# Own values by transposes, ranks by one maximum, a moved one-hot and a share of the own scaling on VectorE, in the last stage of a graph network kernel

## What is computed

```
h = relu(layernorm(x))
q = (h @ Wq + bq).reshape(n, DH, H) * DH ** -0.5      # H = 8 heads, DH = 32
k, v = the same with Wk, bk and Wv, bv
s = einsum('edh,edh->eh', q[row], k[col])
e = exp(s - segment_max(s, row)[row])
a = e / segment_sum(e, row)[row]
x = x + segment_sum(a[:, None, :] * v[col], row).reshape(n, -1) @ Wo + bo
```

## Time and profile before

| | |
|---|---|
| time, median of 3 runs | 3628.44 us (3624.29 to 3637.78) |
| span of the profiled execution | 3555.4 us |
| PE busy | 3183.0 us, 90% |
| DVE busy | 2914.9 us, 82% |
| ACT busy | 2651.2 us, 75% |
| POOL busy | 1969.9 us, 55% |
| mean granted clock of PE | 0.958 |

### The profile page before, as it was taken

The page is one execution under the profiler, slowest core; times in us unless marked ns, Lnnn a source line. Parts: engine busy times, 40 slices in busy tenths (PEclk is TensorE's granted clock), DMA queues, the critical chain, the costliest instruction groups (busy, mean ns, idle before and its releaser), DMA issues. The chain is left out here.

```text
span 3555.4 us, 83958 instructions
## 1 busy us (share of the span) xinstructions
PE 3183.0 (90%) x21026; PEld 2603.3 (73%) x21026; DVE 2914.9 (82%) x8060; ACT 2651.2 (75%) x7851; POOL 1969.9 (55%) x1669
## 2 busy tenths in 40 slices
PE   1699999699998289999999999947999999999998
PEld 0355554477776278888888888836999999999998
DVE  8788887588875378888888888847999999999996
ACT  0688888599997467777777777726888888888886
POOL 0344444155554387777777777725555555555552
PEclk6799999899999689999999999978999999999999
DMA  1455555488886478888888888737666666666663
GB/s 33 145 203 203 201 201 193 175 306 308 307 306 253 166 265 309 310 309 309 308 308 309 308 309 308 290 125 237 236 232 232 232 237 234 233 232 234 233 237 110
DMA packets 335632, 861.24 MB, mean 242 GB/s; under 512 B 98483, under 2 KB 152922, under 8 KB 323018
## 3 DMA queue, kind: packets, MB, share of 16 engines
q1 hardware_dynamic: 241082, 678.75, 53.4%
q0 software_dynamic: 66256, 78.94, 7.5%
q10 hardware_dynamic: 28224, 102.77, 7.1%
HBM read 521.95 MB, written 416.52 MB: 264 GB/s over the span
## 5 line engine op out<-in xcount | busy, mean ns | idle before, releaser
L2191 ACT ACTIVATE e_mine<-e_mine,e_attention 128x32 f32<-128x32 f32 x3136 | 684.8, 308 | 57.8 <-DVE e_attention L2329 57.5
L1715 PE MATMUL c_qkv_ps<-w_qkv_lo,c_ht_hi 128*128 128x256 f16 x2352 | 642.0, 273 | 0.0
L1715 PE MATMUL c_qkv_ps<-w_qkv_hi,c_ht_hi 128*128 128x256 f16 x2352 | 642.0, 273 | 0.0
L1715 PE MATMUL c_qkv_ps<-w_qkv_hi,c_ht_lo 128*128 128x256 f16 x2352 | 641.9, 273 | 0.0
L2146 POOL DMA_INDIRECT e_kv<-kv_table,e_near x392 | 420.9, 1074 | 127.9 <-issue 100.8
L1607 POOL DMA_INDIRECT c_got<-y_table,c_near x392 | 395.0, 1008 | 110.0 <-issue 95.1
L2138 POOL TENSOR_TENSOR e_kv<-e_kv,e_part_of 128x1024 f32<-128x1024 f32 x98 | 188.2, 1921 | 411.2 <-DVE e_part_of L2352 411.2
L2206 PE MATMUL e_out_ps<-w_out,e_mean_t 128*128 128x256 f32 x1568 | 392.8, 380 | 0.0
L776 POOL DMA_INDIRECT dst_slots<-dst_word,dst_goal x240 | 236.6, 986 | 267.5 <-ACT a_hn L812 189.9
L846 PE MATMUL a_h_ps<-a_ht,w_t 128*128 128x512 f32 x784 | 360.8, 603 | 25.1 <-ACT h L794 21.5
L1109 PE MATMUL mix_ps<-w_mix,hb 128*128 128x256 f32 x1568 | 358.1, 382 | 21.2 <-ACT hb L1078 21.2
(11 more groups left out here) (425 smaller groups left out, 8143.7 us busy)
## 6 DMA issues: line engine op xcount, KB each, us to landing
kv_table<-c_kv SPq DMA_DIRECT2D x98, 1024.0 KB, 6.7
h_table<-h ACTq DMA_DIRECT2D x98, 512.0 KB, 2.6
h<-h_table SPq DMA_DIRECT2D x98, 512.0 KB, 4.2
y_table<-y_out ACTq DMA_DIRECT2D x98, 512.0 KB
agg_table<-agg_out SPq DMA_DIRECT2D x98, 512.0 KB
c_agg<-agg_table SPq DMA_DIRECT2D x98, 512.0 KB, 4.3
x_table<-c_x SPq DMA_DIRECT2D x98, 512.0 KB, 2.7
q_table<-c_q SPq DMA_DIRECT2D x98, 512.0 KB, 4.2
```

Of the source, the lines that this page charges most:

```text
L1715: last = nc.tensor.matmul(qkv_ps[n][:, j * D:(j + 1) * D], h[u][:, kc, j * P:(j + 1) * P], wt[:, kc, n * D:(n + 1) * D], start=m == 0, sto ...
L2191: last = nc.scalar.activation(of_head, of_head, ACT.Copy, scale=attention[u][:, j, h, 0:1])
```

## The change

Four things, all in the last stage but for a constant. (1) In each half of the mean the own values are written first, by matmuls with `is_transpose` against the identity, of which the first opens the accumulation; the gathered values are added behind them. The wait for the gathered values stands between the two loops. (2) The prefixes are made with a new constant `raised_h`: `before_h` with 256 on the diagonal. So a slot's own column holds 256 plus its rank and is the row's maximum, and one `reduce_max` over the four rows takes the place of four products with a sum; `layer` compares with 256 to 263. (3) VectorE's order is new: the one-hot is made a step ahead, behind the ranks; sums of scores and spreading come directly behind the attention, then ranks, the one-hot, and the parts. (4) Of the own scaling the fourth row moves from ScalarE (8 activations) to VectorE (one product of 256 elements behind the attention, with its own semaphore). The lower bound of the total (L2323) is gone. The wait for the seen matmul is now a plain `wait_ge`, that for the state a `hold`.

```diff
+RAISE = 256
...
+                    pool.memset(raised_h[:, :], 1.0).then_inc(raising, 1)
+                    pool.wait_ge(raising, 1)
+                    pool.affine_select(out=raised_h[:, :], in_=raised_h[:, :], compare_op=ALU.is_ge, fill=0.0, base=-1,
+                                       pattern=[[1, P]], channel_multiplier=-1).then_inc(raising, 1)
+                    pool.wait_ge(raising, 2)
+                    pool.affine_select(out=raised_h[:, :], in_=raised_h[:, :], compare_op=ALU.not_equal, fill=float(RAISE), base=0,
+                                       pattern=[[-1, P]], channel_multiplier=1).then_inc(const_ready, 1)
...
-                    dve.wait_ge(const_ready, 19)
+                    dve.wait_ge(const_ready, 20)
...
-                            for j in range(kc * 2, kc * 2 + 2):
+                            for j in range(kc * 2, min(kc * 2 + 2, ROWS - 1)):
...
-                    pe.wait_ge(shared, t + 1)
                     pe.wait_ge(own_shared, t * 2 + 2)
+                    pe.wait_ge(own_last, t + 1)
                     wait_past(pe, mean_t_ready, t * 2 + (kc - 1))
                     for j in range(ROWS):
-                        nc.tensor.matmul(mean_ps[kc][:, j * P:(j + 1) * P], kv[w][:, j, D + kc * P:D + (kc + 1) * P], hot[w][:, j, :],
-                                         start=True, stop=False)
-                        last = nc.tensor.matmul(mean_ps[kc][:, j * P:(j + 1) * P], mine[w][:, j, kc * P:(kc + 1) * P],
-                                                ident[:, :], start=False, stop=True)
+                        nc.tensor.matmul(mean_ps[kc][:, j * P:(j + 1) * P], mine[w][:, j, kc * P:(kc + 1) * P], ident[:, :],
+                                         start=j == 0, stop=False, is_transpose=True, skip_group_check=True)
+                    pe.wait_ge(shared, t + 1)
+                    for j in range(ROWS):
+                        last = nc.tensor.matmul(mean_ps[kc][:, j * P:(j + 1) * P], kv[w][:, j, D + kc * P:D + (kc + 1) * P], hot[w][:, j, :],
+                                                start=False, stop=True, skip_group_check=True)
                     last.then_inc(mean_ready, 1)
...
-                            last = nc.tensor.matmul(prefix_ps[:, j, :], before_h[:, :], hot_h[s][:, j, :], start=True, stop=True)
+                            last = nc.tensor.matmul(prefix_ps[:, j, :], raised_h[:, :], hot_h[s][:, j, :], start=True, stop=True)
...
+                def peaks(at):
+                    t, u = ring_tile(at), at[1] % 2
+                    dve.wait_ge(seen_ready, t + 1)
...
+                def normalise(at):
+                    t, (w, n), u = ring_tile(at), in_ring(at, RING), at[1] % 2
+                    dve.wait_ge(weight_ready, t + 1)
+                    hold(dve, state_loaded[w], n * 16 + 16)
+                    v.tensor_tensor(weight[u][:, :, :, 0], weight[u][:, :, :, 0], state[w][:, :, WEIGHTS:STATE], ALU.mult).then_inc(totalling, 1)
+                    dve.wait_ge(totalling, t * 2 + 1)
+                    v.reduce_sum(total[u][:, :, :], weight[u][:, :, :, :], axis=AX.X).then_inc(totalling, 1)
+                    dve.wait_ge(totalling, t * 2 + 2)
+                    v.reciprocal(inverse[u][:, :, :], total[u][:, :, :]).then_inc(inverse_ready, 1)
+                    dve.wait_ge(inverse_ready, t + 1)
+                    wait_past(dve, edge_ready, t - 1)
+                    wait_past(dve, own_shared, t * 2 - 2)
+                    wait_past(dve, own_last, t - 1)
+                    v.tensor_tensor(attention[u][:, :, :, :], weight[u][:, :, :, :],
+                                    inverse[u][:, :, :].unsqueeze(3).to_broadcast([P, ROWS, H, LAYERS + 1]), ALU.mult).then_inc(attention_ready, 1)
+                    dve.wait_ge(attention_ready, t + 1)
+                    dve.wait_ge(mine_loaded[w], n * 16 + 16)
+                    own = mine[w][:, ROWS - 1, :].rearrange("p (h d) -> p h d", h=H)
+                    v.tensor_tensor(own, own, attention[u][:, ROWS - 1, :, 0].unsqueeze(2).to_broadcast([P, H, DH]),
+                                    ALU.mult).then_inc(own_last, 1)
+
+                def ranks(at):
+                    t, s, u = ring_tile(at), in_ring(at, SHORT)[0], at[1] % 2
+                    dve.wait_ge(prefix_ready, t + 1)
+                    v.reduce_max(rank[u][:, :], prefix_ps[:, :, :], axis=AX.X).then_inc(ranked, 1)
+                    dve.wait_ge(ranked, t + 1)
+                    wait_past(dve, chosen, t - (SHORT - 1))
+                    wait_past(dve, layered_ready, t - (SHORT - 1))
+                    v.tensor_tensor(layer[s][:, :, :], lane[:, RAISE:RAISE + LAYERS].unsqueeze(1).to_broadcast([P, ROWS, LAYERS]),
+                                    rank[u][:, :].unsqueeze(2).to_broadcast([P, ROWS, LAYERS]), ALU.is_equal).then_inc(layer_ready, 1)
...
                 def step(at):
-                    if at(0) is not None:
...
-                        v.tensor_tensor(hot_h[s][:, :, :], lane[:, 0:P].unsqueeze(1).to_broadcast([P, ROWS, P]),
-                                        slot_lane[:, bass.ds(t * ROWS, ROWS)].unsqueeze(2).to_broadcast([P, ROWS, P]),
-                                        ALU.is_equal).then_inc(hot_h_ready, 1)
                     if at(2) is not None:
-                        t, (w, n), u = ring_tile(at(2)), in_ring(at(2), RING), at(2)[1] % 2
...
+                        peaks(at(2))
                     if at(1) is not None:
...
+                        products(at(1))
                     if at(4) is not None:
                         result(at(4), 0)
                     if at(2) is not None:
...
-                        v.tensor_scalar(total[u][:, :, :], total[u][:, :, :], 0.5, None, ALU.max).then_inc(totalling, 1)
...
+                        normalise(at(2))
+                    if at(1) is not None:
+                        scores(at(1))
                     if at(0) is not None:
...
-                        for j in range(ROWS):
-                            last = v.scalar_tensor_tensor(counted[u][:, j, :], prefix_ps[:, j, :], 1.0, hot_h[s][:, j, :], ALU.mult, ALU.mult,
-                                                          accum_out=rank[u][:, j:j + 1])
-                        last.then_inc(ranked, 1)
...
+                        ranks(at(0))
+                    if at(-1) is not None:
+                        slot_hot(at(-1))
                     if at(2) is not None:
...
+                        parts(at(2))
                     if at(4) is not None:
                         result(at(4), 1)
...
-                over_ring(dve, NT, 0, 4, step)
+                over_ring(dve, NT, 1, 4, step)
```

106 lines of the change are left out of this document (46 added, 60 removed).

## The result

The changed kernel takes 3511.44 us (median of 4 runs, 3509.20 to 3511.95) against 3630.69 for the kernel before (4 runs, 3624.29 to 3637.78): ratio 0.9663, 95% interval 0.9648 to 0.9678, 119 us or 3.4% less.

A forecast was written before the change was run, and what follows sets the result against it. A full TensorE, 11.375 us per tile, was taken as the bound. Turns 85.6 us, less waits 3.7, plus 5 and 0.5 at the ends, less 1.0 in preparation: 86.4 off 3628.4, so 3542.0 us, range 3530 to 3566.

The forecast's parts named there:

- The turns, 0.92 per tile: Mean on TensorE: eight own-value products per tile go from 0.2225 to 0.1075 us each as transposes, saving 0.92 us.
- C: Rival, mean on TensorE: turns stay two pieces each and get no cheaper, only the ends remain, 3624 us; chance 0.05.
- D: Rival, both halves of the mean: the clock falls to 1.2 GHz during the turns, time 3793 us; chance 0.04.
- The additional waits, 0.04 per tile: TensorE's mean: both additional waits together cost 0.04 us per tile, bounds 0 and 0.06, making the step 10.50 us.
- VectorE's sum: VectorE's work per step in the last stage: from 10.80 to 9.71 us, 0.8 below TensorE.
- rival B: VectorE's L2304 meets GpSimd's L2138 in each step and slows from 0.46 to 1.52 us: 3631 us, no change; chance 0.04.
- 0.6 spare: TensorE's seen matmul: VectorE's parts operation it waits for ends at 9.0, the matmul starts at 9.65, 0.6 us spare.
- A: Rival: the ring through `e_out_ps` becomes the bound; 3556 us if the release comes 0.15 later, 3575 with 0.35; chance 0.14.
- The ring that I called tightest: Seen matmul, mask, peak, q products, half 0 of the result, freeing `e_out_ps`: covered by only 0.05 us.
- ScalarE isn't the bound before or after: ScalarE in the last stage: 9.6 us of work per step, less 1.75 for 8 of 32 activations, never the bound.
- The ends: Tail gains 5 us (2.6 from own-scaling waits, 2.8 from six halves), head 0.5, preparation loses 1.0.
- 73 us around the span: Outside the profiled span of 3555.4 us: the runs' median 3628.44 holds 73 us more, untouched by the change.

The follow-up runs named there:

- e3: Changed kernel with the mean of the kernel before (own values by identity matmuls), all other edits kept: 3552.90 us, ratio 0.9990 to the kernel before.
- h3: Changed kernel with the fourth row's own scaling back on ScalarE: 3491.76 us, ratio 0.9817 to the kernel before.
- e2: Kernel before with only the mean changed, own values as transposes ahead of the gathered ones: 3503.64 us, ratio 0.9851 to the kernel before.
- g3: Changed kernel with the ranks again by four products with a sum instead of one maximum: 3529.59 us, ratio 0.9708 to the kernel before.
- g4: Changed kernel with VectorE's product of edge shares ahead of the one-hot, its sum left behind it: 3504.23 us, ratio 0.9640 to the kernel before.
- k1: Kernel before, unchanged, profiled in a series where it takes about 3635 us: 3632.03 us.
- g1: Changed kernel repeated unchanged, in a series where the kernel before takes about 3635 us: 3507.83 us, ratio 0.9648 to the kernel before.
- h1: Kernel before, unchanged, as control in a series where it takes about 3555 us: 3554.97 us.

## Why the prediction was right and wrong

*TensorE is the bound, and a full one: right in the main.* It is busy 900.00 of 900 us before and after, and e3 shows the converse: 81 us less of VectorE's work in the stretch give 4 us in all. But the sign that I named for being wrong, less than 99% busy, would not have shown a miss: h3 loses 26.8 us at 99.7%, and the long step of the changed kernel stands in a stretch with 100%.

*The turns, 0.92 per tile: right.* They are one piece each (784 records), 0.43 to 0.44 for four; the step without stalls is 10.417 where the sum had 10.455 without waits. The rival that they stay two pieces (C) fell, and so did the clock (D): 1.00 throughout. The Trainium skill, "TensorE: Matmul & The Clock Gate", Part 4: PE-mode transpose, says that the high clock doesn't engage on turns; the trace doesn't bear this out for eight turns a tile among matmuls.

*The additional waits, 0.04 per tile: no price to be seen.* The short step of 10.417 is 0.04 under the 10.455 without any. The one long step in six brings the average to 10.455, 0.045 under the forecast 10.50: 4 us of 93 steps.

*VectorE's sum: its operations right, the sum 0.34 us too low.* Predicted and measured: one-hot 0.63 and 0.69; maximum 0.68 and 0.68; own scaling 0.42 and 0.425; L2316 (before L2304) 0.46 and 0.459, at most 0.525, so rival B fell. It fell by luck in part: I had L2148 end at 0.9 of the step and L2316 start at 1.3, and measured they are 1.49 and 1.28, counted from the turns at 2649.05. But VectorE is idle 0.41 us ahead of the mask in each step, where nearly 1 was forecast. So it is occupied for 10.05 us and not 9.71; 0.18 of the difference is idle time ahead of the one-hot that no wait covers (0.14 to 0.26 in a step), 0.06 its duration. Without the edits to VectorE a step was to be above TensorE, 10.80 to 10.88; e2 has 10.83.

*"0.6 spare" for the seen matmul: a term mis-sized.* Counted from the turns at 2649.05, the edge product starts at 8.89 and ends at 9.31, not 8.6 and 9.0, since 0.19 us stand ahead of the attention and 0.14 to 0.26 ahead of the one-hot; L2277 starts at 9.58 where 9.65 was forecast. The time from the product's end to L2277's start is 0.26 to 0.38 at five positions and 0.15, which is the wait's own, at the sixth, and this wait, not the ring through `e_out_ps` (A), sets the long step. The ring that I called tightest has no wait of TensorE in the stretch. With the old ranks it stops every step (g3). g4 shows the mechanism by removing it.

*"ScalarE isn't the bound before or after": wrong as an argument, harmless in the result.* I read its busy share and its first 16 activations only, and followed no path from the exponential back to the attention. h3 shows a ring through VectorE's attention, two sets of 16 activations and the exponential at 10.69 us, 0.27 above TensorE's step. The 8 activations that move are what opens it: 26.8 us of the gain, to which the prediction gave nothing but the 2.6 us of two waits in the tail.

*The ends: nearly right.* The stage gained 91.5 us in the 3555 kind, of which 85.6 are 0.92 a step and 5.9 are at the ends (forecast 5.5, with the tail's 2.6 and 2.8 booked as 5). In the tail the own scaling's 1.3 us waits are gone and shorter ones for the mean copy stay:

```profile
3446.45 0.28 PE L2214 MATMUL e_out_ps<-b_out,all_b 128*128 128x256 bf16 x1 [0.84 <-ACT e_mean_t L2193]
```

The preparation: L524 at 8.0 instead of 7.25, plus 0.75 where 1.0 was forecast.

*"73 us around the span, which the change doesn't touch": this step failed.* Time less span is 2 us in every run. The profile of before came from the 3555 kind and the three times from the 3635 kind, and I booked the difference as fixed. In the 3555 kind the forecast would have been 3555.4 - 86.4 + 2 = 3471 and the measured time is 3465: right to 6 us, though the moved scaling, worth 26.8 us there, had been given a price in the tail alone. In the 3635 kind the kernel before holds 38 us more ahead of the stage, which the change indeed leaves alone, and 36 us more inside the stage, which the changed kernel doesn't lose: k1's 1195.3 less g1's 1070.7 is 124.6 us. Ahead of the stage 5.0 are given back (2435.9 against 2430.9), and the spans give 3626.2 - 3506.6 = 119.6, the gain of the result. So the 33 missing us are the 36 that the kernel before loses in the stage (1195.3 against h1's 1159.6), plus the 4 by which the stage gained more than forecast in the 3555 kind (91.5 against 87.4), less the 3 by which the changed kernel's stage grows in the 3635 kind, less the 4 more that are given back ahead of the stage (5.0 where 1.0 was forecast). That this last sum closes is arithmetic on single profiles; the 36 us themselves are measured, their cause is open but for the late increments above. What spoke for two kinds ahead of time: the profiled span lies 69 us below the lowest of the three times, which differ among themselves by 14.
